# FFN stages of a single-core megakernel: order of gates and weight splits, a wait ahead of one set of weight loads, and where the gathered rows are summed

## The reference, cut to what matters

```python
xt = layernorm(x).reshape(-1, 512)                     # 512 tokens
scores = softmax(xt @ gate_w.T)                        # 8 experts
_, idx = top_k(scores + gate_bias, 2)
weights = take_along_axis(scores, idx, axis=1)
for e in range(8):
    gate_e = sum(where(idx == e, weights, 0), axis=1)
    h = silu(xt @ w1[e].T) * (xt @ w3[e].T)
    y = y + gate_e[:, None] * (h @ w2[e].T)
z = silu(xt @ sw1.T) * (xt @ sw3.T) @ sw2.T             # shared, inner width 1024
x = x + y + z
```

## Time and profile before

| | |
|---|---|
| Runs | 545.13, 549.85, 552.69 us; median 549.85 |
| Profiled execution, its own time | 544.2 us |
| Its span, first to last instruction | 542.4 us |
| PE busy | 472.5 us (87%) |
| DVE busy | 399.8 us (74%) |
| ACT busy | 330.3 us (61%) |
| POOL busy | 298.6 us (55%) |
| Weight loads `wst<-in_ffw` | 51 of 1024 KB |
| Mean granted TensorE clock | 0.974 of full |

### The profile page before, as it was taken

One profiled execution on the slowest core, in us unless ns is written; L12 is line 12 of the kernel. 1 busy time (PEld: TensorE's weight loads), 2 busy tenths in 40 slices (PEclk: granted clock), 3 DMA queues, 4 the chain that ended last, 5 costly groups with the idle time before them and its releaser, 6 DMA issues.

```text
span 542.4 us, 15769 instructions
## 1 busy us (share of the span) xinstructions
PE 472.5 (87%) x6731; PEld 329.3 (61%) x6731; DVE 399.8 (74%) x603; ACT 330.3 (61%) x360; POOL 298.6 (55%) x278
## 2 busy tenths in 40 slices
PE   0479999889899899999989838877999999999993
PEld 0136666667666666766675616533878788787641
DVE  3476878667787767787835898785579999999417
ACT  4255767667777666776572535572378888888310
POOL 2348899899989899998686504381001111010041
PEclk9999999999999999999999967989999999999998
DMA  8697997978999878866996341198559999997144
GB/s 263 136 288 246 255 260 216 265 162 235 255 254 256 241 197 215 241 174 172 290 417 252 118 155 63 52 411 346 187 196 394 418 417 416 415 416 291 40 114 139
DMA packets 48249, 133.94 MB, mean 247 GB/s; under 512 B 6450, under 2 KB 31282, under 8 KB 37426
## 3 DMA queue, kind: packets, MB, share of 16 engines
q1 hardware_dynamic: 44500, 120.88, 69.2%
q0 software_dynamic: 3680, 12.06, 6.1%
HBM read 96.74 MB, written 11.01 MB: 199 GB/s over the span
## 4 chain that ended last, share of the span: by engine, by line
PE 43%; DVE 33%; DMA 8%; issue 7%; POOL 5%; ACT 2%; SPq 1%; DVEq 0%; ACTq 0%; POOLq 0%
DVE mx L696 11%; DVE ws L770 9%; PE bank L1003 8%; PE bank L968 8%; PE bank L1012 7%; PE bank L988 6%; DMA kt<-in_keysT 4%; POOL xs_rows L660 3%; DMA wst<-in_ffw 3%; DVE rden L713 2%; PE bank L1126 2%; PE bank L1127 2%; PE bank L1128 2%; DVE hf L908 1%; DMA xs_rows<-ao_wproj,posu 1%
## 5 line engine op out<-in xcount | busy, mean ns | idle before, releaser
L696 DVE TENSOR_REDUCE mx<-bank 128x1 f32<-128x512 f32 x256 | 163.1, 686 | 66.1 <-PE bank L968 65.4
L614 POOL TENSOR_TENSOR ps<-pt 128x512 f32<-128x512 f32 x128 | 160.0, 1279 | 10.8 <-PE bank L1012 5.6
L457 ACT ACTIVATE pt<-bank 128x1024 f32<-128x1024 f32 x128 | 125.8, 1023 | 65.9 <-PE bank L988 65.8
L770 DVE SCALAR_TENSOR_TENSOR ws<-wst,ws 128x2048 f16<-128x2048 f32 x51 | 116.9, 2312 | 2.8 <-ACT ws L501 2.7
L968 PE MATMUL bank<-kstk,q 96*128 96x512 f16 x256 | 96.4, 407 | 24.9 <-DVE mx L696 7.8
L501 ACT ACTIVATE ws<-wst 128x2048 f16<-128x2048 f32 x48 | 90.6, 1904 | 10.5 <-PE bank L1209 6.6
L587 POOL TENSOR_TENSOR kl<-kt,kh 128x512 f16<-128x512 f32 x62 | 70.6, 1163 | 23.6 <-ACT kh L422 23.6
L988 PEld LDWEIGHTS bank<-q,kstk 98*128 98x128 f16 x1024 | 68.1, 100 | 22.8 <-issue 4.5
L1141 PE MATMUL bank<-xt,ws 128*128 128x128 f16 x480 | 81.2, 219 | 0.6 <-DVE hf L908 0.6
L1142 PE MATMUL bank<-xt,ws 128*128 128x128 f16 x480 | 81.2, 219 | 0.0
L1143 PE MATMUL bank<-xt,ws 128*128 128x128 f16 x480 | 81.2, 219 | 0.0
(11 more groups left out here) (161 smaller groups left out, 644.0 us busy)
## 6 DMA issues: line engine op xcount, KB each, us to landing
wst<-in_ffw SPq DMA_DIRECT2D x51, 1024.0 KB, 10.7
kt<-in_keysT SPq DMA_DIRECT2D x16, 1024.0 KB, 6.1
kstk<-kh SPq DMA_DIRECT2D x128, 128.0 KB, 3.5
v<-in_vals SPq DMA_DIRECT2D x16, 1024.0 KB, 9.0
kstk<-kl SPq DMA_DIRECT2D x64, 128.0 KB, 3.9
xs_rows<-biases SPq DMA_DIRECT2D x15, 256.0 KB, 3.0
x_tok<-xs_rows POOLq DMA_DIRECT2D x15, 256.0 KB, 8.6
ys_rows<-xn POOLq DMA_DIRECT2D x15, 256.0 KB, 6.5
```

The lines of the kernel that those rows point to most:

```text
L457: act.activation(pt[:, n % 4, :, :, :].rearrange("p j a t -> p (j a t)"), bank[:, 2 * (n % 2):2 * (n % 2) + 2, :].rearrange("p j n -> p (j ...
L614: pool.tensor_tensor(ps2[:, n % 4, :, :], pt[:, n % 4, 0, :, :], pt[:, n % 4, 1, :, :], ALU.add)\
L696: dve.tensor_reduce(mx[:, a, q:q + 1], bank[:, 4 + k % 2, :], AX.X, ALU.max).then_inc(m_taken, 1)
L770: dve.scalar_tensor_tensor(ws[:, home_of(q), 1, m, :, :].rearrange("p c n -> p (c n)"), wst[:, q % 2, m, :, :].rearrange("p c n -> p (c n) ...
```

## The change

Four edits.

1. `splits_at` gives the shared stages other pairs: none in stage 0; (1,0) in stage 1; (1,1), (2,0) in stage 2; (2,1), (1,2), (2,2) in stage 3; (3,0), (3,1) in stage 4. Pair (3,2) moves from stage 4 to stage 5 (block 0). ACT and DVE both read this list.
2. SP waits for the whole scatter ahead of the loads (3, m), the weights of block 1.
3. In stages 0 and 1 DVE runs `hidden_low(n)` right behind `gated(n)`, ahead of `place_tokens` and of the splits.
4. The gathered rows of batch 0 are summed ahead of `gated(22)`; those of batches 1 to 3 each ahead of the final step of the batch before.

```diff
--- before.py
+++ after.py
@@ -75,9 +75,8 @@
 def splits_at(n):
     kind, k, it = STAGES[n]
     if kind == "shared":
-        return {0: [(1, 0), (1, 1)], 1: [(1, 2), (2, 0)], 2: [(2, 2), (2, 1)], 3: [(3, 0)],
-                4: [(3, 1), (3, 2)]}.get(n, [])
-    return ([(seq_of_block(k + 1), m) for m in (1, 2) if 0 < k < NB - 1]
+        return {1: [(1, 0)], 2: [(1, 1), (2, 0)], 3: [(2, 1), (1, 2), (2, 2)], 4: [(3, 0), (3, 1)]}.get(n, [])
+    return ([(seq_of_block(k + 1), m) for m in (1, 2) if 0 < k < NB - 1] + [(seq_of_block(1), 2)] * (k == 0)
             + [(seq_of_block(k + 2), 0) for _ in range(1) if k + 2 < NB])
 
 
@@ -387,6 +386,7 @@
 
         for m in range(3):
             load_w(2, m, 1)
+        sp.wait_ge(xs_in, 16 * K_TOP * B)
         for m in range(3):
             load_w(3, m, 3)
         for k, m in ((2, 0), (2, 2), (2, 1), (3, 0), (3, 1), (3, 2), (4, 0)):
@@ -919,14 +919,31 @@
             dve.tensor_copy(xt[:, k % 2, :, :], half_bank(6).rearrange("p (c n) -> p c n", c=2 * C)).then_inc(xt_done, 1)
 
         choose_experts()
+        def combine(b):
+            dve.wait_ge(yg_in[b], 16 * K_TOP)
+            link(dve.scalar_tensor_tensor(x2[:, b, :], yg[:, K_TOP * b, :], gk[:, 0, b:b + 1], x2[:, b, :], ALU.mult,
+                                          ALU.add))
+            link(dve.scalar_tensor_tensor(x2[:, b, :], yg[:, K_TOP * b + 1, :], gk[:, 1, b:b + 1], x2[:, b, :],
+                                          ALU.mult, ALU.add))
+
+        def finish(b):
+            dve.wait_ge(y_ready, b + 1)
+            dve.scalar_tensor_tensor(x1[:, b, :], bank[:, b, :], 1.0 / WS, x2[:, b, :], ALU.mult, ALU.add)\
+                .then_inc(x3_done, 1)
+
         for n, (kind, k, it) in enumerate(STAGES):
             todo = splits_at(n)
+            if n == len(STAGES) - 1:
+                combine(0)
             gated(n)
+            if n < 2:
+                hidden_low(n)
             if n == 0:
                 place_tokens()
             for q, m in todo[:1]:
                 split_low(q, m)
-            hidden_low(n)
+            if n >= 2:
+                hidden_low(n)
             if n == FRONT - 1:
                 slots(0)
                 slots(1)
@@ -934,16 +951,10 @@
                 slots(k + 2)
             for q, m in todo[1:]:
                 split_low(q, m)
-        for b in range(B):
-            dve.wait_ge(yg_in[b], 16 * K_TOP)
-            link(dve.scalar_tensor_tensor(x2[:, b, :], yg[:, K_TOP * b, :], gk[:, 0, b:b + 1], x2[:, b, :], ALU.mult,
-                                          ALU.add))
-            link(dve.scalar_tensor_tensor(x2[:, b, :], yg[:, K_TOP * b + 1, :], gk[:, 1, b:b + 1], x2[:, b, :],
-                                          ALU.mult, ALU.add))
-        for b in range(B):
-            dve.wait_ge(y_ready, b + 1)
-            dve.scalar_tensor_tensor(x1[:, b, :], bank[:, b, :], 1.0 / WS, x2[:, b, :], ALU.mult, ALU.add)\
-                .then_inc(x3_done, 1)
+        for b in range(1, B):
+            combine(b)
+            finish(b - 1)
+        finish(B - 1)
 
 
     @blk.tensor
```

## The result

The changed kernel takes 540.94 us (median of 20 runs, 536.4 to 549.53) against 548.33 for the kernel before (20 runs, 543.92 to 559.61): a ratio of 0.9869, 95% interval 0.9843 to 0.9896, so 5.7 to 8.6 us faster, which by the 2% bounds of the prediction is still the same time. The profiled execution has a span of 537.4 us against 542.4.

A forecast was written before the change was run, and what follows sets the result against it. The scatter, its indirect DMAs held by DVE's splits and full DMA queues, was taken to bound the stretch before `up_block(0)`. Terms -7.3 + 2.8 + 1.7 + 0.5 - 1.6 = -3.9 us gave a median of 546.0, range 539.5 to 552.5.

The forecast's parts named there:

- scatter landed: Stages 0 to 3: the scatter's last DMA lands at 365.1 instead of 372.43; -7.3 us.
- lag to `up_block(0)`: From scatter landed to `up_block(0)`: the late weight load (3,0) lengthens it from 9.7 to 12.5 us; +2.8 us.
- clock in `up_block(0)`: First block: after a second PE idle stretch, 3.4 us at half rate; +1.7 us, or 0.
- stream: Weight loads deferred behind the scatter: free DMA time covers them, with a small loss late; +0.5 us (0 to 3).
- end: Last sums and final steps: reordered gathered sums let the last store go earlier; -1.6 us.
- three cases for the eighth: Scatter: landed at 363.0, 365.1 or 367.9, by whether the third and eighth DMAs pass ahead of a split.
- SP's wait: Weight loads behind the scatter: none in flight, so the last scatter DMA lands 1.8 us after its end.
- The early scatter: Rival, chance 0.2: eighth DMA passes ahead of split (2,1), (3,0) lands in 5.1 us, clock holds; -9.1, so 540.8 us.
- the stream becomes the bound: Rival, chance 0.1: deferred weight loads come back as ACT's waits after stage 14; -1.4, so 548.5 us.
- the end doesn't gain: Rival, chance 0.05: gathers land after 527.3 and `combine(0)` holds `gated(22)`; -2.3, so 547.6 us.
- The port holds DVE too: Rival, chance 0.05: scatter DMAs also push back DVE's splits, scatter landed at 367.9; -1.1, so 548.8 us.
- The slower rival: Chance 0.15: late scatter, (3,0) landing in 7.2 us and no free DMA time outweigh the gain; +2.1, so 552.0 us.

The follow-up runs named there:

- e8: The changed kernel without SP's wait and with DVE's `slots(0)` ahead of split (3,0) in stage 4; ratio 0.9814 to before.
- e12: The changed kernel without SP's wait and with `slots(0)` ahead of split (3,0), the same kernel as e8 run again; ratio 0.974 to before.
- e1: The kernel before with the new lists of splits and the early `hidden_low` in stages 0 and 1, no SP wait, old end; ratio 0.9813 to before.
- e4: The changed kernel without SP's wait; ratio 0.9769 to before.
- e5: The changed kernel, but after the scatter SP issues only (3,0) and holds all other weight loads until the first block's rows land; ratio 0.9809 to before.
- e3: The kernel before with the new end alone (the reordered gathered sums); ratio 0.9936 to before.
- e11: The changed kernel without SP's wait, the same kernel as e4 run again; ratio 0.9795 to before.
- e2: The kernel before with SP's wait alone; ratio 0.9987 to before.
- e7: The kernel before with the new lists of splits alone; `hidden_low`, SP and the end as before; ratio 0.9879 to before.
- e6: The changed kernel with SP waiting for only the first four of eight scatter DMAs; ratio 0.995 to before.

## Why the prediction was right, and where its sizes were off

The median forecast was 546.0 with a range of 539.5 to 552.5; measured 540.9. The sign and the range held, the gain was about double: by the markers 8.4 us, where the sum said 3.9. The forecast started from the median of the three runs that it had, 549.85; over 20 runs it is 548.33, so 1.5 of the 5.1 us between 546.0 and 540.9 are in the starting point.

| term | forecast | measured |
|---|---|---|
| scatter landed | -7.3 | 15.75 - 25.39 = -9.6 |
| lag to `up_block(0)` | +2.8 | 12.58 - 9.67 = +2.9 |
| clock in `up_block(0)` | +1.7 | 0 |
| stream | +0.5 | 146.86 - 146.78 = +0.1 |
| end | -1.6 | 10.36 - 12.13 = -1.8 |
| sum | -3.9 | -8.4 |

- *The scatter.* The rule "a DMA ends 0.92 us after the split it meets" held for every row. Of the two cases left open for the third and the eighth DMA both fell on the early side: the forecast's early ends, counted from 347.04, are 3.7, 5.9, 8.7, 11.5, 12.8 and 14.0; measured 3.7, 5.9, 8.7, 11.5, 12.7 and 14.0. The term was mis-sized by 2.3 us, nearly all because I took the middle of three cases for the eighth. It starts 0.25 us before split (2,1) (363.50 and 363.75); it took 0.96 us in all eleven profiles with the new lists.
- *SP's wait.* "With SP's wait no weight load is in flight, so the landing takes what the first one's did" gave the right number, but the wait is for the most part not the reason, and here the reasoning failed. The landing after the last end is 1.75 us with the wait and 2.0 to 2.7 without (e8 and e12 at the ends, e1 and e4 2.4). The new order alone keeps most of the loads off the last scatter DMA; the wait adds 0.6 us to the gain up to the landing (e4), and then costs 3.8 us between it and `up_block(0)` (12.58 against 8.82 in e4). I had credited it with the whole fall of the landing, 6.24 - 1.8 = 4.4 us, and had no rival in which the change would be better without it.
- *The lag.* 12.5 forecast, 12.58 measured, but by another path. I let the three row loads slow the weight load (6.5 us) and kept the row load at its 4.16. It was the other way: (3,0) landed in 5.1 us, and the row load took 7.07. By the path that I had added up `slots(0)` ended at 376.80, which with 0.5 for the transposes would have been S + 11.1; the row load and the low clock in `down(3)` made it S + 12.58. That the sum came to the same is luck. e5 shows the size of the contention: 5.5 us with one weight load beside the row load.
- *The clock.* The fall was there, in `down(3)` as before, 3.4 us at 1.2 GHz, and not in `up_block(0)`. The second idle stretch that was to bring it didn't exist, since `down(3)` itself came so late. This follows from the lag's wrong path; 1.7 us too many. With the same order and no wait (e1, e4) PE's only hole is 1.34 us, and the clock stays at 1.00.
- *The early scatter.* This rival (0.2) is the one that came true: the eighth DMA passed, (3,0) landed in 5.1 us, and the clock held in `up_block(0)`. Its sum was -9.1 us, measured -8.4; the lag was 1.5 us longer than its 1.4, because of the slowed row load, which it left out too. That its 540.8 lies within 0.2 us of the measured 540.94 is partly the starting point that was 1.5 us too high.
- *The stream.* The deferred loads were absorbed as worked out (DMA share 0.96 in place of 0.60 in the same 28 us from `up_block(0)`, PE never waiting there; the +0.1 is far below the 1.6 us by which this stretch differs between profiles). The rival "the stream becomes the bound" is not what happened.
- *The end.* Right: 1.36 us of margin against 1.3 forecast, 1.8 us gained against 1.6. The rival "the end doesn't gain" fell with e3.
- *The port holds DVE too.* It fell: split (1,0), with two inputs in SBUF, starts at 353.21, just after DMA three (353.18), 0.61 us behind `hidden_low(1)` as usual, and takes its 2.29 us. The Trainium skill's rule (section "Who interferes with whom" of "SBUF — State Buffer") is borne out in the direction in which GpSimd waits, also by gathers five and eight (1.30 us beside DVE's sums, 1.43 beside `hidden_low(22)`), and in no row in the other by more than a few hundredths of a microsecond.
- *The slower rival*, "SP's wait costs more than the scatter gains", had half of the mechanism and the wrong balance. The late weight load costs 1.5 us (e5 against e4); the other 1.6, the slowed row load with the low clock behind it, it didn't name. Against these 3.2 us at `up_block(0)` stand 9.6 of gain up to the landing, nearly all of which the order brings by itself.

The lowest ratio of a kernel with all its loads is that of the changed one without SP's wait and with `slots(0)` ahead of split (3,0): 0.974 (0.9692 to 0.9789) and 0.9814 (0.9745 to 0.9883) of before, in e12 and e8. Its intervals overlap those of e4 and e11, which lack the wait alone; that `up_block(0)` starts 1.5 us earlier is shown, that the whole is faster than e4 isn't.

## What to carry to other kernels

A wait that keeps bulk loads out of a small transfer's way releases them all at once when it ends, on top of the next small transfer; look at what stands in the queues at the moment each small DMA on the path is issued, and at which buffer release sets the bulk loads free. When a change makes two edits for the same end, price each one alone, the case "the other already does it" included. And where the stretch ahead of a change varies by as much as the change is worth, count in both profiles from a marker just ahead of it.

## What the runs showed of the hardware

- A two-input SBUF operation of DVE holds the issue of POOL's indirect DMAs even when no weight load is in the DMA queues (e2: 2.45 to 2.50 us against 0.96), and lets one through between two operations, however short the gap: each ends 0.92 us after the start of the DVE row behind the split. `hidden_low`, a `tensor_tensor` with both inputs in SBUF, does the same (gather eight: 1.43 us against 0.94), and `gated`, with one input in PSUM, doesn't (the last scatter DMA starts inside it and takes 0.96).
- A 256 KB row load of POOL takes 2.9 us when no weight load is issued in its first 1.7 us (e4), 5.5 with one beside it (e5) and 7.1 with two and soon six (changed kernel); a 1 MB weight load of SP issued just ahead of three of them lands in 4.8 to 5.1 us (e2, e5, changed kernel), no later than alone (5.1). So POOL's transfers bore the contention, not the first of SP's; the second, issued 0.4 us behind it, took 8.4.
- The sixth scatter DMA, which starts with two weight loads just issued, took 8.9 us to land in e6, against 4.3 in the changed kernel with none in the queues; the eighth 6.2 against 2.7.
- In this stretch the granted clock was 0.50 (1.2 GHz) for about 3 us or more after PE had idled 2.55 us (e7), 2.80 (changed kernel) and 6.37 (e6), and stayed at 1.00 after 1.19 and 1.52 (e5) and 1.34 (e1, e4).
